# A GRU over gathered item rows: 12 raw steps in place of 10, a ring of 16 steps in place of 12

## The chip, the cores and the metric

The kernel runs on one core of one Trainium2 chip. The metric is the device time of one execution in microseconds. Three runs of the kernel before took 1093.35, 1089.58 and 1090.4 us, so the median is 1090.4 us. Engines are named as in the profile: PE is TensorE (PEld its weight loads), DVE is VectorE, ACT is ScalarE, POOL is GpSimd, SP is SyncE.

## The reference

512 sequences of 200 item numbers go through one GRU layer of width 128 and then through a dense layer with softmax over 100 classes. The item table has 12,500 rows of 128 floats.

```python
x = emb[item_seq]                       # [512, 200, 128], f32
mask = item_seq != 0
def step(h, x_t, m_t):
    mx = x_t @ W + b_i                  # W, U: [128, 384]
    mh = h @ U + b_r
    z = sigmoid(mx[:, :D] + mh[:, :D])
    r = sigmoid(mx[:, D:2*D] + mh[:, D:2*D])
    hh = tanh(mx[:, 2*D:] + r * mh[:, 2*D:])
    return where(m_t, z * h + (1 - z) * hh, h)
# 200 steps in order, h starts at 0
softmax(h_last @ Wout + bout)
```

## The kernel before

The batch of 512 is four blocks of 128. Blocks 0 and 1 are chain 0, blocks 2 and 3 chain 1, and the two chains take turns on the engines. The state of a chain is a tile of 128 x 256 floats, features by sequences. A step needs, for every sequence, the row of its item.

The work has three stages.

1. **Building two tables in DRAM.** SP loads the transposed item table into the SBUF tile `arena`. PE turns it back tile by tile (L323), ACT and DVE copy the tiles to `turned`, and SP stores them as `rows` (item rows of 128 floats, L210 to L216). PE also multiplies each tile by W (L318), ACT and DVE copy the products to `proj` (L453, L517), and SP stores them as `table` (rows of 384 floats, already multiplied by W, L221 to L230). A mask is built in: item 0 points at a row that pins the update gate.
2. **Raw steps**, t = 0 to RAW - 1. They use `rows`, which is complete before `table` is. POOL gathers 128 rows per block with an indirect DMA (L284, 4 per step) into the tile `raw`. PE transposes them (L351), ACT copies the result to `xT` (L474), and PE multiplies by W for the three gates (L358, L359, L362) and adds the pin (L365).
3. **Table steps**, t = RAW to 199. POOL gathers rows of `table` (L302, 4 per step, each 128 rows of 384 floats) into `arena`, which by then serves as a ring of RING steps. PE transposes the rows straight into the sums of the three gates (L377, 12 transposes per step); no multiplication by W is left.

In both kinds of step PE multiplies the state by U (L383 reset gate, L385 candidate, L389 update gate), ACT computes r (L478), z (L480) and the candidate (L482), and DVE does five operations per chain (L541, L544, L546, L549, and L552, which writes the new `h`).

Every engine has its own instruction stream in program order, and semaphores join them. What orders the work around the change is POOL's stream: its 4 x RAW raw gathers, then one wait for all stores of `table` (L289 to L291), then the gathers for the table steps. Table step number n = t - RAW uses ring slot n % RING. From n = RING on, POOL waits until PE has transposed the rows that the slot held before:

```python
if n >= RING:
    pool.wait_ge(s_free[c], n - RING + 1)
```

A raw step and a table step share the semaphore of a slot, so for n < RAW the table gather also waits for the raw gather of the same number (L301).

POOL's stream is written out for all steps. On PE, ACT and DVE the table steps are a loop of TURNS = (200 - RAW) // RING turns of RING steps, and the LEFT remaining steps stand behind it: 15 turns and 10 steps before.

Of the kernel before, what the change touches and what calls it, by code (L numbers as in the profile page):

```python
# [14 lines left out]

CHAINS = ((0, 1), (2, 3))
WIDTH = 2 * P
RAW = 10
RING = 12
CHUNK = 8  # L20
HALF = CHUNK // 2
GROUP = 4
# [5 lines left out]
def gru(nc: bass.Bass, item_seq, emb_cols, W, U, b_i, b_r, Wout, bout, out):  # L28
# [17 lines left out]
    CLASSES = Wout.shape[1]  # L46
    assert D == P and GATES == 3 * D and BATCH == BLOCKS * P and 1 <= RAW <= RING
    TURNS = (STEPS - RAW) // RING
    LEFT = STEPS - RAW - TURNS * RING
    BOTH = range(len(CHAINS))  # L50
# [6 lines left out]
    assert TILES == CHUNKS * CHUNK + 1 and TILES == GROUPS * GROUP + 1 and 0 < REST < P  # L57
    assert ITEMS <= RING * BLOCKS * GATES

# [5 lines left out]
    with ExitStack() as ctx:  # L65
        def sb(name, shape, dt=F32):
            return ctx.enter_context(nc.sbuf_tensor(name, shape, dt))

        def sem(name):
            return ctx.enter_context(nc.semaphore(name))  # L70

        def per_chain(name):
            return [sem(f"{name}{c}") for c in BOTH]
# [3 lines left out]

        arena = sb("arena", [P, RING * BLOCKS * GATES])
        raw = sb("raw", [P, RAW * BLOCKS * D])
        turned = [sb(f"turned{q}", [P, CHUNK, D]) for q in range(STAGES)]  # L80
# [15 lines left out]
        SEQS = BLOCKS * STEPS  # L96
        assert 4 * SEQS <= RAW * BLOCKS * D

# [7 lines left out]
        copy_f = sb("copy_f", [P, 1])  # L106
        masked = sb("masked", [P, RAW * BLOCKS], BF16)
        pins = sb("pins", [P, P], BF16)
# [59 lines left out]

        s_slot = [[sem(f"slot{s}_block{k}_gathered") for k in range(BLOCKS)] for s in range(RING)]
        s_x = per_chain("x_turned")  # L170
# [439 lines left out]
```

## Time and profile before

| | us |
|---|---|
| median of three runs | 1090.4 |
| profiled execution, its own time | 1093.43 |
| its span, first to last instruction | 1091.6 |
| outside the span (1093.43 - 1091.6) | 1.83 |
| POOL busy in the span | 803.7 |
| PE busy in the span | 981.0 |
| first raw gather, first table gather, last table gather (starts) | 40.19, 99.88, 1074.58 |

The profile gives each engine's busy time and the idle time ahead of its instructions. A busy share is no proof that an engine sets the pace: PE's share is the highest, but it is a mean over stretches in which different things come last. One gather is two times: how long POOL needs to issue it (the duration of the instruction), and how long until its rows have landed (another view gives that).

### The profile page before, as it was taken

The page shows a single profiled execution, that of the slowest core. Times are in us where ns is not written, and L with a number is a line of the kernel's source. Part 1 is how long each engine was busy: PE and PEld are TensorE (multiplying, and loading weights), DVE is VectorE, ACT ScalarE, POOL GpSimd, SP SyncE. Part 2 cuts the span into 40 slices and gives each one's busy share as a digit, 9 for nine tenths or more (in the row PEclk, how much of TensorE's full clock was granted, in tenths as well). Part 3 has the DMA queues.
Part 4 walks back from the last instruction along what each step waited for, and adds up shares of the span by engine and source line. Part 5 has one row for each costly group of instructions (what it writes and reads, how often), then busy time and mean ns, then how long its engine had stood idle before and what let it go on. Part 6 is the DMA issues. An engine that isn't in the chain of part 4 may idle for free.

```text
span 1091.6 us, 15880 instructions
## 1 busy us (share of the span) xinstructions
PE 981.0 (90%) x5185; PEld 756.4 (69%) x5185; DVE 862.6 (79%) x2074; ACT 577.7 (53%) x1288; POOL 803.7 (74%) x820
## 2 busy tenths in 40 slices
PE   6899999999999999999999999888888888888885
PEld 5556887777777777777777776666666666666664
DVE  3344778888888888888888888888888888888886
ACT  3334655555555555555555555555555555555554
POOL 6574777777777777777777777777777777777773
PEclk9899999999999999999999999999999999999998
DMA  9997555555555555555555555555555555555552
GB/s 359 378 360 262 159 157 153 153 152 154 151 155 152 153 153 153 154 152 152 153 156 152 153 152 154 153 152 151 154 152 155 153 153 154 153 152 154 152 155 81
DMA packets 59696, 185.75 MB, mean 170 GB/s; under 512 B 14830, under 2 KB 16408, under 8 KB 59672
## 3 DMA queue, kind: packets, MB, share of 16 engines
q0 software_dynamic: 49920, 152.09, 49.4%
q1 hardware_dynamic: 8356, 32.47, 7.5%
q10 hardware_dynamic: 1396, 0.91, 0.3%
q8 instruction: 9, 0.15, 0.1%
q14 instruction: 15, 0.12, 0.0%
HBM read 159.35 MB, written 26.07 MB: 170 GB/s over the span
## 4 chain that ended last, share of the span: by engine, by line
DVE 29%; DMA 23%; PE 16%; issue 12%; ACT 11%; POOL 9%; DVEq 0%; SPq 0%; POOLq 0%; ACTq 0%
DMA arena<-table,row_table 21%; ACT cand L482 10%; DVE rh L541 10%; POOL arena L302 9%; DVE zc L549 9%; DVE pre L544 9%; PE bank L318 5%; PE bank L377 4%; DMA rows<-turned 1%; PE bank L383 1%; DVE h L552 1%; PE bank L389 1%; PE bank L385 1%; PE bank L358 1%; PE bank L362 1%
## 5 line engine op out<-in xcount | busy, mean ns | idle before, releaser
L302 POOL DMA_INDIRECT arena<-table,row_table x760 | 744.4, 979 | 241.0 <-issue 178.2
L377 PE MATMUL bank<-ident,arena 128*128 128x128 f32 x2280 | 346.5, 277 | 64.3 <-DMA arena<-table,row_table 63.9
L377 PEld LDWEIGHTS bank<-ident,arena 128*128 128x128 f32 x2280 | 269.4, 141 | 141.6 <-DMA arena<-table,row_table 103.0
L482 ACT ACTIVATE cand<-pre,bi 128x256 f32<-128x256 f32 x400 | 203.3, 508 | 280.4 <-DVE pre L544 280.4
L383 PE MATMUL bank<-h,U_sb 128*128 128x256 f32 x800 | 261.6, 409 | 22.5 <-DVE h L552 4.9
L549 DVE SCALAR_TENSOR_TENSOR zc<-z,cand 128x256 f32<-128x256 f32 x400 | 171.2, 428 | 92.9 <-ACT cand L482 92.9
L389 PE MATMUL bank<-h,U_sb 128*128 128x256 f32 x800 | 239.3, 381 | 0.0
L385 PE MATMUL bank<-h,U_sb 128*128 128x256 f32 x800 | 238.6, 380 | 0.0
L478 ACT ACTIVATE r<-bank,b_gates 128x256 f32<-128x256 f32 x400 | 185.1, 463 | 83.3 <-PE bank L383 82.2
L541 DVE SCALAR_TENSOR_TENSOR rh<-bank,br,r 128x256 f32<-128x256 f32 x400 | 191.8, 479 | 44.6 <-ACT r L478 34.2
L480 ACT ACTIVATE z<-bank,b_gates 128x256 f32<-128x256 f32 x400 | 189.3, 473 | 69.8 <-PE bank L389 69.8
L552 DVE TENSOR_TENSOR h<-zh,zc 128x256 f32<-128x256 f32 x400 | 172.9, 432 | 13.8
L544 DVE TENSOR_TENSOR pre<-rh,bank 128x256 f32<-128x256 f32 x400 | 168.2, 420 | 13.8
L383 PEld LDWEIGHTS bank<-h,U_sb 128*128 128x128 f32 x800 | 120.1, 190 | 74.0 <-DVE h L552 73.9
L546 DVE TENSOR_TENSOR zh<-z,h 128x256 f32<-128x256 f32 x400 | 169.7, 424 | 0.4 <-ACT z L480 0.4
L385 PEld LDWEIGHTS bank<-h,U_sb 128*128 128x128 f32 x800 | 152.4, 190 | 20.7
L389 PEld LDWEIGHTS bank<-h,U_sb 128*128 128x128 f32 x800 | 137.3, 190 | 37.6 <-DVE pre L544 3.1
L318 PE MATMUL bank<-W_sb,arena 128*128 128x384 f32 x198 | 70.5, 510 | 3.7 <-ACT proj L453 3.7
L318 PEld LDWEIGHTS bank<-W_sb,arena 128*128 128x128 f32 x198 | 38.6, 201 | 28.5 <-ACT proj L453 4.4
L517 DVE COPY proj<-bank 128x384 f32<-128x384 f32 (+1 forms) x49 | 27.2, 557 | 39.0 <-PE bank L318 33.7
L284 POOL DMA_INDIRECT raw<-rows,row_table x40 | 38.0, 950 | 20.2 <-issue 11.9
L453 ACT COPY proj<-bank 128x384 f32<-128x384 f32 x50 | 23.8, 479 | 45.0 <-PE bank L318 39.1
(55 smaller groups left out, 165.8 us busy)
## 6 DMA issues: line engine op xcount, KB each, us to landing
table<-proj SPq DMA_DIRECT2D x24, 768.0 KB, 3.9
arena<-table,row_table POOLq DMA_INDIRECT x760, 3.1
arena<-in_L_rec_emb SPq DMA_DIRECT2D x12, 512.0 KB, 10.1
rows<-turned SPq DMA_DIRECT2D x12, 512.0 KB, 10.7
raw<-rows,row_table POOLq DMA_INDIRECT x40, 4.0
seq<-in_r_item_seq ACTq DMA_DIRECT2D x1, 400.0 KB, 10.3
table<-proj SPq DMA_DIRECT2D x2, 192.0 KB
out_probs<-probs SPq DMA_DIRECT2D x1, 200.0 KB, 2.6
```

The source lines that it names most:

```text
L302: pool.indirect_dma_start(ring_rows(s, k), None, table, bass.IndirectOffsetOnAxis(row_table[:, t, k:k + 1], 0)).then_inc(s_slot[s][k], 16)
L377: last = pe.matmul(dst[:, i * P:(i + 1) * P], ring_row(s, k, g), ident[:, :], start=(i == 0), stop=False, is_transpose=True, skip_group_ch ...
L383: pe.matmul(reset_sum[c], U_sb[:, D:2 * D], h[c][:, :], start=False, stop=True, skip_group_check=True).then_inc(s_reset[c], 1)
L385: pe.matmul(cand_h[c], U_sb[:, 2 * D:3 * D], h[c][:, :], start=False, stop=True, skip_group_check=True).then_inc(s_cand[c], 1)
L389: pe.matmul(update_sum[c], U_sb[:, 0:D], h[c][:, :], start=False, stop=True, skip_group_check=True).then_inc(s_update[c], 1)
L478: act.activation(r[c][:, :], reset_sum[c], ACT.Sigmoid, bias=b_gates[:, 1:2]).then_inc(s_r[c], 1)
L480: act.activation(z[c][:, :], update_sum[c], ACT.Sigmoid, bias=b_gates[:, 0:1]).then_inc(s_z[c], 1)
L482: act.activation(cand[c][:, :], pre[c][:, :], ACT.Tanh, bias=bi[:, 2:3]).then_inc(s_tanh[c], 1)
L541: dve.scalar_tensor_tensor(out=rh[c][:, :], in0=cand_h[c], scalar=br[:, 2:3], in1=r[c][:, :], op0=ALU.add, op1=ALU.mult).then_inc(s_rh[c], 1)
L544: dve.tensor_tensor(pre[c][:, :], rh[c][:, :], cand_x[c], ALU.add).then_inc(s_pre[c], 1)
L549: dve.scalar_tensor_tensor(out=zc[c][:, :], in0=z[c][:, :], scalar=1.0, in1=cand[c][:, :], op0=ALU.subtract, op1=ALU.mult).then_inc(s_zc[c ...
L552: dve.tensor_tensor(h[c][:, :], zh[c][:, :], zc[c][:, :], ALU.subtract).then_inc(s_h[c], 1)
```

## The change

RAW goes from 10 to 12 and RING from 12 to 16. Two constants change, and everything else follows from them.

```diff
-RAW = 10
-RING = 12
+RAW = 12
+RING = 16
```

Steps 10 and 11 become raw steps: 48 raw gathers in place of 40, and 752 table gathers in place of 760. `raw` grows from 20 to 24 KB per partition and `arena` from 72 to 96 KB. The loop on PE, ACT and DVE has 11 turns of 16 steps and 12 steps behind it.

On POOL, the number of gathers of each kind at the end of the index work and behind it (`raw` and `arena` are the targets, `rows` and `table` the two tables):

```order
 L269 TENSOR_TENSOR raw<-raw 128x800
 L272 TENSOR_TENSOR raw<-raw 128x800
 L274 CAST row_table<-raw 128x800
-L284 DMA raw<-rows,row_table 128x128 x40
-L302 DMA arena<-table,row_table 128x384 x760
+L284 DMA raw<-rows,row_table 128x128 x48
+L302 DMA arena<-table,row_table 128x384 x752
 L65 UNCONDITIONAL_BRANCH
```

Eight gathers move from behind the wait for the table's stores to ahead of it; the total stays 800.

On POOL, where the first gathers that wait for a free ring slot stand (`rows_transposed0` and `1` are PE's signals that a chain's rows have been transposed). Before:

```order
L302 DMA arena<-table,row_table 128x384 [waits slot9_block3_gathered]
L302 DMA arena<-table,row_table 128x384 x8
L302 DMA arena<-table,row_table 128x384 [waits rows_transposed0]
L302 DMA arena<-table,row_table 128x384
L302 DMA arena<-table,row_table 128x384 [waits rows_transposed1]
```

And now:

```order
L302 DMA arena<-table,row_table 128x384 [waits slot11_block2_gathered]
L302 DMA arena<-table,row_table 128x384 [waits slot11_block3_gathered]
L302 DMA arena<-table,row_table 128x384 x16
L302 DMA arena<-table,row_table 128x384 [waits rows_transposed0]
L302 DMA arena<-table,row_table 128x384
L302 DMA arena<-table,row_table 128x384 [waits rows_transposed1]
```

The first 48 table gathers (40 that wait for a raw gather and 8 that wait for nothing) were free of the wait for a slot; now the first 64 are (48 and 16).

On PE, at the end of the raw steps, the first half of the first added raw step (each of the two steps has two such halves, one per chain):

```order
 L362 MATMUL bank<-xT,W_sb 128x256
 L365 MATMUL bank<-pins,masked 128x128 x2
+L351 MATMUL bank<-ident,raw 128x128 x2
+L383 MATMUL bank<-h,U_sb 128x256
+L385 MATMUL bank<-h,U_sb 128x256
+L389 MATMUL bank<-h,U_sb 128x256
+L358 MATMUL bank<-xT,W_sb 128x256
+L359 MATMUL bank<-xT,W_sb 128x256
+L362 MATMUL bank<-xT,W_sb 128x256
+L365 MATMUL bank<-pins,masked 128x128 x2
```

Two steps of PE's work change from six transposes and three multiplications per chain to the form above, so PE reaches the first table step later by what a raw step takes, twice.

## Rows read from the trace of the kernel before

**Rows 1.** The page: span, busy time and count of each engine.

```profile
span 1091.6 us, 15880 instructions
PE 981.0 (90%) x5185; PEld 756.4 (69%) x5185; DVE 862.6 (79%) x2074; ACT 577.7 (53%) x1288; POOL 803.7 (74%) x820
```

**Rows 2.** Waits of POOL: waiting line, releaser, us in total, times, longest us.

```profile
POOL arena L302 <- issue: 178.2, 585, 0.3
POOL arena L302 <- PE bank L377: 53.0, 174, 0.3
POOL arena L302 <- DMA table<-proj: 9.8, 1, 9.8
```

**Rows 3.** Timeline of POOL: start, us, line, operation, [idle before, releaser].

```profile
85.40 0.94 POOL L284 DMA_INDIRECT raw<-rows,row_table  x1 [0.30 <-issue]
...
89.15 0.94 POOL L284 DMA_INDIRECT raw<-rows,row_table  x1 [0.30 <-issue]
99.88 0.95 POOL L302 DMA_INDIRECT arena<-table,row_table  x1 [9.79 <-DMA table<-proj]
...
160.29 0.95 POOL L302 DMA_INDIRECT arena<-table,row_table  x1 [0.30 <-issue]
...
1074.58 0.95 POOL L302 DMA_INDIRECT arena<-table,row_table  x1 [0.30 <-issue]
```

**Rows 4.** Line 302 by itself: count, durations, first and last start; landing times.

```profile
L302 POOL DMA_INDIRECT arena<-table,row_table x760: 942/946/1197, 99.9 to 1074.6; - x190
...
DMA to landing us min/median/max: 2.9/3.1/4.8
```

**Rows 5.** Stretches of PE's line 377: stretch, length, busy (count), PEclk, DMA, GB/s.

```profile
155.00:660.00 505.00, 177.68 (x1302) 155.37 (x1302) 1.00 0.54 153
680.00:1060.00 380.00, 153.18 (x886) 102.94 (x886) 1.00 0.54 153
```

**Rows 6.** The same two stretches, POOL alone.

```profile
155.00:660.00 505.00, 385.40 (x393) 1.00 0.54 153
680.00:1060.00 380.00, 290.12 (x296) 1.00 0.54 153
```

**Rows 7.** Chain that ended last, in order of time, around 664 us.

```profile
663.55 0.84 PE bank L377 x6
...
664.46 0.95 POOL arena L302
...
665.71 3.06 DMA arena<-table,row_table
```

**Rows 8.** Timeline of DVE's line 552, the new state.

```profile
108.33 0.42 DVE L552 TENSOR_TENSOR h<-zh,zc 128x256 f32<-128x256 f32 x1
...
155.19 0.45 DVE L552 TENSOR_TENSOR h<-zh,zc 128x256 f32<-128x256 f32 x1
...
160.26 0.49 DVE L552 TENSOR_TENSOR h<-zh,zc 128x256 f32<-128x256 f32 x1
...
269.68 0.49 DVE L552 TENSOR_TENSOR h<-zh,zc 128x256 f32<-128x256 f32 x1
272.25 0.42 DVE L552 TENSOR_TENSOR h<-zh,zc 128x256 f32<-128x256 f32 x1
...
1081.29 0.43 DVE L552 TENSOR_TENSOR h<-zh,zc 128x256 f32<-128x256 f32 x1
```

**Rows 9.** Timeline of PE, the first and the last table transposes.

```profile
156.06 0.82 PE L377 MATMUL bank<-ident,arena 128*128 128x128 f32 x6
...
1071.86 0.90 PE L377 MATMUL bank<-ident,arena 128*128 128x128 f32 x3 [2.31 <-DMA arena<-table,row_table]
...
1079.01 0.82 PE L377 MATMUL bank<-ident,arena 128*128 128x128 f32 x6
```

**Rows 10.** Stretches, all engines (PE, PEld, DVE, ACT, POOL), around the table's last stores.

```profile
40.00:90.00 50.00, 48.26 (x141) 28.17 (x142) 19.96 (x36) 17.59 (x37) 37.91 (x40) 0.93 0.93 355
90.00:100.00 10.00, 8.91 (x35) 5.54 (x34) 2.85 (x6) 3.39 (x8) 0.21 (x2) 1.00 0.80 302
```

## The prediction

> **What bounds the kernel now.** I read the page first, then POOL's waits, POOL's timeline, and one pair of stretches on PE and POOL. By the page PE is busiest (90%) and POOL third (74%) [rows 1], which by itself would make PE the suspect. POOL's waits say otherwise. Ahead of its 760 table gathers POOL idles in three ways: 585 times for "issue", 178.2 us in all, that is 0.305 us each; 174 times with PE named as releaser, 53.0 us, that is also 0.305 us each and never over 0.3; and once for the table's stores, 9.8 us [rows 2]. A gap that is the same with and without a releaser is POOL's own gap between two gathers, so no gather ever waited for a ring slot. POOL issues one gather after the other from 99.88 to 1074.58 us: (1074.58 - 99.88) / 759 = 1.284 us each [rows 3]. The only hole in its stream of 800 gathers is the wait for the stores.
>
> PE's pace and POOL's pace are close, and the stretches tell which is slower. There are 12 transposes of line 377 in a step, so from 155 to 660 us a step takes 505 / (1302 / 12) = 4.65 us, and from 680 to 1060 us 380 / (886 / 12) = 5.15 us [rows 5]. POOL needs 4 x 505 / 393 = 5.14 us for the gathers of a step in the first stretch and 4 x 380 / 296 = 5.14 us in the second [rows 6]. POOL is thus the slower one all the way. At first PE eats up the lead that POOL gained during the raw steps; at 664 us the lead is gone, the chain that ends last goes over from PE to gathers and their landings [rows 7], and from there PE's step is POOL's. The end of the kernel is therefore the time at which POOL may begin with table gathers, plus their number times 1.284 us, plus a tail.
>
> **The change part by part.**
>
> *Eight more raw gathers ahead of the wait.* The raw gathers from 85.40 to 89.15 us stand (89.15 - 85.40) / 3 = 1.25 us apart [rows 3]. The last one of before starts at 89.15; eight more start from 90.40 to 99.15, and POOL is ready for the first table gather at 100.40 us. Before, the stores released it at 99.88. So the eight fill the hole of 9.79 us (0.30 of which is the usual gap) and overrun it by 0.52 us. If the stores land later because of them, that counts only from 100.40 on; rival B prices it.
>
> *Eight fewer table gathers behind it.* 8 x 1.284 = 10.27 us. From both parts the last gather starts 10.27 - 0.52 = 9.75 us sooner, at 1064.83 us. Landing, the last steps and the softmax (1091.6 - 1074.58 = 17.0 us) stand behind the last gather in both kernels, and I cost them as equal.
>
> *Two raw steps in place of table steps on PE, ACT and DVE.* From the second to the tenth raw step the new state of chain 0 comes every (155.19 - 108.33) / 8 = 5.86 us [rows 8], against 4.65 us of a table step. Two steps cost 2 x 1.21 = 2.42 us. POOL's slower pace hides them. Had PE kept 4.65 us from step 10 (state at 160.26 us) to step 199, that state would come at 160.26 + 189 x 4.65 = 1039.1 us; it came at 1081.29 [rows 8], so PE has 42.2 us to spare. After the change it has 42.2 - 2.4 - 9.75 = 30.0 us. If POOL stopped setting the pace, the 2.42 us would count in full.
>
> *The ring of 16.* In the kernel before it buys nothing, since no gather waited for a slot. With 12 raw steps it is needed. The first gather that waits for a slot is the 49th, at 160.29 us [rows 3], and PE clears the first slot at 156.06 + 0.82 = 156.88 us [rows 9], 3.4 us ahead. Two more raw steps move the clearing to 156.88 + 2 x 5.86 = 168.6 us. With 12 slots POOL would come to the 49th gather at about 100.40 + 160.29 - 99.88 = 160.8 us and stand for 7.8 us, most of the gain. With 16 slots the first gather that waits is the 65th, at about 160.8 + 16 x 1.284 = 181.3 us, 12.7 us behind the clearing. So the ring is worth zero by itself and keeps 7.8 us here. In later steps PE is faster than POOL and the margin only grows.
>
> *Other edits.* The mask for 12 steps has 48 columns in place of 40 and lies ahead of the wait for the item rows: nothing. A loop of 11 turns in place of 15 saves four jumps back; at a jump the state of one chain comes 272.25 - 269.68 = 2.57 us after the other's in place of about 4.65 / 2 = 2.33 [rows 8], so four jumps are 1.0 us of PE's time, which POOL's pace hides. What a loop body longer by a third costs at the jump, no row shows: between -1.0 us (four jumps fewer, were PE the bound) and rival A's price. I take 0, the side of the nearest row, since the present body of 12 x 12 transposes and more jumps for 0.24 us.
>
> The Trainium skill (Runtime: NRT & Kernel Launch, Instruction fetch mechanics) says that a taken branch to a target outside the fetched window of instructions makes the engine wait for a fetch. The row on the jump, 0.24 us, shows no such wait; by the row the sum stays as it is, by the rule it becomes rival A's.
>
> *Sum.* 1093.43 - 9.75 = 1083.7 us for an execution like the profiled one, which is 3.0 us above the median of the runs (1090.4) and close to the slowest of them. The difference applied to the median: 1090.4 - 9.75 = 1080.6 us.
>
> **The rivals.**
>
> *A, slower: the longer loop body is fetched anew at each jump.* One mechanism on PE, ACT or DVE, 11 times. It begins to show only when it uses up the 30.0 us to spare, at 30.0 / 11 = 2.7 us per turn, and makes the kernel slower by over 0.3% (3.3 us) from (30.0 + 9.75 + 3.3) / 11 = 3.9 us per turn. As its price I take the longest landing of a transfer in the rows, 4.8 us [rows 4]: 11 x 4.8 - 30.0 = 22.8 us, and 1080.6 + 22.8 = 1103 us. For it: 12 steps have been shown to be cheap, 16 have not. Against it: the 0.24 us. Chance 0.05.
>
> *B, smaller gain: the added gathers delay the stores.* From 90 to 100 us the DMA engines moved 302 GB/s at a share of 0.80, from 40 to 90 us 355 GB/s at 0.93 [rows 10]. Eight gathers bring 8 x 128 x 512 bytes = 0.52 MB into that stretch, 52 GB/s over 10 us, which makes 354 and uses up what was free. At worst the last store lands later by all of it, 0.52 MB / 355 GB/s = 1.5 us: release at 101.4 us, 1.0 us behind 100.40, gain 8.75, time 1081.7 us. At best nothing moves, since 354 is still below the 355 that was reached. Chance 0.11.
>
> The Trainium skill (DMA: Bandwidth & Descriptors, Issuing engines are not separate DMA queues) says that DMAs started by different engines run on the same 16 DMA engines and interleave. The two stretches agree in that gathers and stores together stayed near 355 GB/s; by the rows the sum stays, and by the rule taken alone B's 1 us comes off the gain.
>
> *C, no change: what POOL gives back early is lost at a new wait.* Say the gathers of the two added steps land late and the table gathers of slots 10 and 11, which now wait for them, hold POOL; or gathers slow down in the wider `arena`: 10 us over 752 gathers would take 0.013 us each, less than their spread of 942 to 1197 ns [rows 4]. Time 1090.4 us. Against it: those waits come 40 gathers, about 50 us, after the raw gathers were issued, and landings take 3.1 us in the median. Chance 0.07.
>
> A small gain beside these belongs to the forecast's own range. Near the end one gather's rows let PE wait 2.31 us, and PE's last transposes start at 1079.01 us, though the last gather could have landed at 1074.58 + 3.1 = 1077.7 us [rows 3, 4, 9]. If that late landing is chance and does not come again, the end is up to 1.3 us earlier.
>
> **How the numbers follow.** Forecast 0.77, A 0.05, B 0.11, C 0.07. Forecast 1080.6 us. Its own range goes down to 1077.5 (the 1.3 us, and 1.8 for the spread of the runs) and up to 1083.7 (an execution like the profiled one). With B and its spread the range is 1077.5 to 1085.0; A and C, 0.12, stay outside. A difference under 0.3% of the time, 3.3 us, cannot be told from no change. Faster: 0.77 + 0.11 = 0.88; same: 0.07; slower: 0.05.
>
> **What would show it.** After the change POOL's idle time ahead of its first table gather should be about 0.3 us (up to 1.3 under B) in place of 9.79, that gather should start at 100.4 us (to 101.4), and the spacing of table gathers should stay at 1.284 us. The chain should go over to gathers later: POOL's lead at a given step is greater by 9.75 + 2.42 = 12.2 us, PE closes 5.14 - 4.65 = 0.49 us per step, 25 steps or 116 us, so near 664 + 2 + 116 = 782 us. The last table gather should start near 1065 us. The prediction is wrong if POOL stands anywhere for a slot or a landing, if gathers come more than 1.29 us apart, or if PE waits for anything but gathers in the last 200 us.

## The result: 1081.7 us after 1090.0 us, as POOL's hole was filled

The changed kernel took 1081.68 us in the median (1080.71 to 1082.67, four runs), the kernel before 1090.0 us beside it; the ratio is 0.9917, 95% interval 0.9895 to 0.9939, so the change is small but clear of no change. Measured once more beside the experiments it was 1082.19 us against 1091.67, ratio 0.9909 (0.9893 to 0.9926). The forecast was 1080.6 us, range 1077.5 to 1085.0.

The profiled execution of the changed kernel took 1081.61 us. The first lines of its page, which answer to [rows 1]:

```profile
span 1079.8 us, 15857 instructions
PE 982.1 (91%) x5201; PEld 757.4 (70%) x5201; DVE 860.4 (80%) x2074; ACT 571.7 (53%) x1292; POOL 804.8 (75%) x820
```

The busy times hardly differ. What changed is where POOL stands idle. Its waits in the changed kernel (waiting line, releaser, us in total, times, longest), to be read against [rows 2]:

```profile
POOL arena L302 <- issue: 186.1, 611, 0.3
POOL arena L302 <- PE bank L377: 42.9, 141, 0.3
```

The third row of before, the 9.8 us for the table's stores, has no successor. POOL's timeline, against [rows 3] (start, us, line, operation, [idle before, releaser]):

```profile
39.26 1.20 POOL L284 DMA_INDIRECT raw<-rows,row_table  x1 [7.28 <-DMA rows<-turned_last]
...
98.19 0.94 POOL L284 DMA_INDIRECT raw<-rows,row_table  x1 [0.30 <-issue]
99.44 1.07 POOL L302 DMA_INDIRECT arena<-table,row_table  x1 [0.31 <-issue]
...
1065.22 0.95 POOL L302 DMA_INDIRECT arena<-table,row_table  x1 [0.30 <-issue]
```

The first table gather follows the last raw gather after 0.31 us, POOL's usual gap, and the last gather starts 9.36 us sooner than before. Line 377 on PE, against [rows 5] (stretch, length, PE busy (count), PEld busy (count), PEclk, DMA share, GB/s), and the place where the chain that ends last goes over to gathers, against [rows 7] (start, us, what):

```profile
166.00:730.00 564.00, 198.74 (x1458) 173.88 (x1457) 1.00 0.53 153
790.00:1010.00 220.00, 88.63 (x513) 59.73 (x513) 1.00 0.53 153
```

```profile
740.90 0.76 PE bank L377 x6
741.85 0.95 POOL arena L302
743.10 3.23 DMA arena<-table,row_table
```

PE still takes 564 / (1458 / 12) = 4.64 us for a step while it has a lead to eat up, and 220 / (513 / 12) = 5.15 us once it works on each gather as it lands. The lead lasts until 742 us in place of 664.

### The profile page after: what moved, and what is told of

It is laid out like the page before. It is cut to its first block, busy times and chain, and to the rows that moved or that the text cites. A ratio compares the mean times of both kernels' runs of the same rounds, so it can differ in the third digit from the quotient of the medians.

```text
span 1079.8 us, 15857 instructions
## 1 busy us (share of the span) xinstructions
PE 982.1 (91%) x5201; PEld 757.4 (70%) x5201; DVE 860.4 (80%) x2074; ACT 571.7 (53%) x1292; POOL 804.8 (75%) x820
## 4 chain that ended last, share of the span: by engine, by line
DVE 33%; DMA 19%; PE 16%; ACT 13%; issue 12%; POOL 6%; DVEq 0%; SPq 0%; POOLq 0%; ACTq 0%
DMA arena<-table,row_table 16%; ACT cand L482 12%; DVE rh L541 11%; DVE zc L549 10%; DVE pre L544 10%; POOL arena L302 6%; PE bank L318 5%; PE bank L377 3%; DMA rows<-turned 1%; PE bank L383 1%; DVE h L552 1%; PE bank L389 1%; PE bank L385 1%; PE bank L358 1%; PE bank L359 1%
## 5 line engine op out<-in xcount | busy, mean ns | idle before, releaser
L377 PE MATMUL bank<-ident,arena 128*128 128x128 f32 x2256 | 334.5, 276 | 49.4 <-DMA arena<-table,row_table 49.3
L318 PE MATMUL bank<-W_sb,arena 128*128 128x384 f32 x198 | 67.6, 494 | 1.5 <-ACT proj L453 1.5
L284 POOL DMA_INDIRECT raw<-rows,row_table x48 | 45.5, 949 | 21.6 <-issue 14.3
## 6 DMA issues: line engine op xcount, KB each, us to landing
rows<-turned SPq DMA_DIRECT2D x12, 512.0 KB, 10.4
seq<-in_r_item_seq ACTq DMA_DIRECT2D x1, 400.0 KB, 10.4
```

The costliest lines, as they stand in the source:

```text
L377: last = pe.matmul(dst[:, i * P:(i + 1) * P], ring_row(s, k, g), ident[:, :], start=(i == 0), stop=False, is_transpose=True, skip_group_ch ...
```

## The experiments

Theory: POOL's stream of 800 gathers sets the end. Its length without holes is fixed, so the time is the start of the stream, plus that length, plus any hole, plus a tail. Rivals: the deeper ring or the shorter count of loop turns gives the gain; each raw step saves its table gathers without limit; PE sets the end.

Start, hole, last gather, stream and tail are from the one profiled execution of each kernel, the medians from all its runs (us). Each ratio is to the kernel before as it ran in the same group: 1090.0 us for the changed kernel, 1091.0 for the next four, 1091.67 for the four after them, 1091.63 for the last two.

| kernel | first gather | hole | last gather | stream less hole | tail | median | ratio (95%) |
|---|---|---|---|---|---|---|---|
| before, 10 raw, ring 12 | 40.19 | 9.49 | 1074.58 | 1024.9 | 17.0 | 1090.0 | |
| changed, 12 raw, ring 16 | 39.26 | 0 | 1065.22 | 1026.0 | 14.6 | 1081.68 | 0.9917 (0.9895 to 0.9939) |
| 12 raw, ring 12 | 39.59 | 6.58 | 1072.88 | 1026.7 | 17.4 | 1088.93 | 0.9979 (0.9968 to 0.999) |
| 10 raw, ring 16 | 39.80 | 8.26 | 1075.39 | 1027.3 | 14.5 | 1091.79 | 1.0002 (0.9991 to 1.0013) |
| 11 raw, ring 16 | 40.21 | 4.17 | 1070.88 | 1026.5 | 14.5 | 1085.23 | 0.9941 (0.9925 to 0.9957) |
| 14 raw, ring 15 | 39.37 | 0 | 1066.09 | 1026.7 | 15.7 | 1083.64 | 0.9933 (0.9917 to 0.9949) |
| the change again | 39.31 | 0 | 1064.32 | 1025.0 | 14.9 | 1082.19 | 0.9909 (0.9893 to 0.9926) |
| 12 raw, ring 14 | 40.25 | 0 | 1067.42 | 1027.2 | 15.4 | 1083.88 | 0.9924 (0.9909 to 0.9939) |
| rows given | 32.30 | 0 | 1057.45 | 1025.2 | 15.5 | 1075.79 | 0.9858 (0.9838 to 0.9878) |
| rows given, index on DVE | 21.54 | 3.10 | 1049.88 | 1025.2 | 15.1 | 1066.81 | 0.9766 (0.9748 to 0.9783) |
| the same, 14 raw, ring 18 | 22.54 | 0 | 1048.20 | 1025.7 | 14.8 | 1065.63 | 0.9762 (0.9749 to 0.9776) |
| the change, loop ends early | 39.55 | 0 | 1064.67 | 1025.1 | 14.9 | 1081.43 | 0.9909 (0.9894 to 0.9924) |

The hole is the idle time less the usual gap of 0.30 us; the tail is the span less the start of the last gather. In the twelve profiles the stream without its hole took 1024.9 to 1027.3 us, or 1.283 to 1.286 us a gather; what makes this spread of 2.4 us, no run shows.

**12 raw steps with the ring of 12** (the ring part undone).

```diff
-RING = 16
+RING = 12
```

> 12 raw steps with the old ring of 12. Theory (POOL's stream of 800 gathers without a hole sets the end, and the ring of 16 only keeps it free of a hole): the 49th table gather, due near 160.1 us, waits for the first slot, which PE clears near 164.7 us, so a hole of 4 to 9 us opens on POOL there and the kernel takes 1086 to 1090 us. Rival (the ring is idle, the raw steps give the whole gain): no hole, 1081.7 us as with the change.

POOL's timeline at the 49th table gather, and PE's transposes that clear the first slot:

```profile
159.13 0.94 POOL L302 DMA_INDIRECT arena<-table,row_table  x1 [0.30 <-issue]
166.95 0.94 POOL L302 DMA_INDIRECT arena<-table,row_table  x1 [6.88 <-PE bank L377]
168.20 0.95 POOL L302 DMA_INDIRECT arena<-table,row_table  x1 [0.30 <-issue]
```

```profile
165.86 0.82 PE L377 MATMUL bank<-ident,arena 128*128 128x128 f32 x6
```

The hole of the kernel before is gone at 99.8 us and comes back at 160 us, 6.88 us long, released within 0.3 us of the end of PE's first transposes. Most of the gain goes with it: 1088.93 us. The raw steps alone are worth 0.2%.

**10 raw steps with the ring of 16** (the ring part alone), **11 raw steps** (half of the raw part) and **14 raw steps** (twice the raw part, with 15 slots, which fit).

```diff
-RAW = 12
+RAW = 10        # then 11, and 14 with RING = 15
```

> 10 raw steps with the ring of 16. Theory: no gather ever waited for a slot, so nothing changes, 1090 us (within 0.3%), with a hole of 6 to 10 us ahead of the first table gather. Rival (the deeper ring or the fewer jumps of the loop give the gain): 1082 us. Rival (a loop body of 16 steps costs a fetch per turn): over 1093 us.

> 11 raw steps, ring of 16. Theory: four gathers fill half of the hole, so the gain is four table gathers, 4 x 1.286 = 5.1 us: 1085 us (1083.5 to 1087, since the hole varies with the time at which the table's stores land). Rival (the gain comes only with a full fill or only from the ring): 1090 or 1082 us.

> 14 raw steps, ring of 15 (16 slots do not fit in SBUF beside them). Theory: the hole is full already, POOL's 800 gathers take the same time in any mix, and PE's two longer steps (2.4 us) are hidden: 1081.7 us within 0.2%, first table gather near 109.4 us and last near 1065 us. Rival 1 (each pair of raw steps saves its eight table gathers): 1071.5 us. Rival 2 (PE's longer raw steps are paid in full): 1084 us.

The wait for the table's stores with 10 and with 11 raw steps, and line 302 by itself with 14 (count, shortest, median and longest in ns, first and last start):

```profile
POOL arena L302 <- DMA table<-proj: 8.6, 1, 8.6
```

```profile
POOL arena L302 <- DMA table<-proj: 4.5, 1, 4.5
```

```profile
L302 POOL DMA_INDIRECT arena<-table,row_table x744: 942/947/1198, 109.8 to 1066.1; - x186
```

The ring alone leaves the hole at 8.6 us and the time where it was (1.0002). Four gathers leave a hole of 4.5 us and give 0.6%, eight give 0.8 to 0.9%, and sixteen give 0.7%, no more than eight: with 14 raw steps the first table gather starts 10.4 us later than with 12 and the last 0.9 us later. Rival 1 of that run (1071.5 us) is out. Its 1083.64 us was 2 us above the changed kernel; the intervals overlap, so whether the two longer steps of PE or the later table gathers cost anything is not settled by the times, but the profile shows no wait of POOL over 0.3 us.

**The change again, and 12 raw steps with a ring of 14.**

```diff
-RING = 16
+RING = 14
```

> The change once more, as the measure for the others of this group. Theory: ratio 0.991 to 0.994 to the kernel before (eight gathers of 1.286 us fewer behind the stores, less what the hole falls short of ten microseconds), so 1082 us. In the profile again one late landing of 4.6 to 4.9 us after the loop's end, with a block of instructions of 16 KB on the DMA engines in the same stretch.

> 12 raw steps, ring of 14. Theory: the first gather that waits for a slot is the 57th, due at 99.4 + 56 x 1.257 = 169.8 us, 5 us after PE clears the slot at 164.7 us, so 14 slots are enough: no hole, the same time as the change within 0.2%. Rival (each slot fewer costs something): half way between 12 and 16 slots, 1085 us.

With 14 slots no gather waits (longest idle of POOL at line 302: 0.3 us), as the 57th gather comes after the slot is clear. The time was 1.7 us above that of 16 slots in the same group (1083.88 and 1082.19), with overlapping intervals. In the profiles the stream started 0.94 us later and was 2.2 us longer, without any hole; that lies within the spread of the column in the table above. Whether two slots fewer cost anything below this spread is open.

**An earlier start of the stream.** If start plus length is the time, an earlier start must pay in full. In the first of two versions the item rows come as an input in row layout, with the zero row and the copies of the last row behind them; turning the table and storing `rows` fall away, and the raw gathers need to wait only for the index work. In the second the index work runs on DVE between the copies of the products. The cut shows the first lines of each part only.

```diff
-def gru(nc, item_seq, emb_cols, W, ...):
+def gru(nc, item_seq, emb_cols, rows, W, ...):
-            for q in range(STAGES):
-                pool.wait_ge(s_rows[q], 16 * len(range(q, CHUNKS, STAGES)))
-            pool.wait_ge(s_rows_last, 16 * 3)
...
-            pool.tensor_copy(item_f, seq[:, :, :]).then_inc(s_idx, 1)
+                dve.tensor_copy(item_f, seq[:, :, :]).then_inc(s_idx, 1)
```

> The change, with the item rows (and the zero row and the 128 copies of the last row) handed over as a further input in row layout, so that the kernel neither turns the table back nor stores the rows; index work stays on POOL. Theory: POOL's stream starts where the index work ends, near 32 us in place of 39.3, and the end moves by the same 7.3 us: 1074.5 us (1073 to 1076). Rival (the end is set by PE, which gets its table earlier by some 20 us): over 10 us less, 1065 us. Rival (the start of the stream does not matter since the stores release it): 1081.7 us.

> As the one with the rows given, and the index work moved from POOL to DVE, between the copies of the products. Theory: the stream starts near 20 to 24 us, 15 to 19 us before that of the change, and the end moves by as much: 1063 to 1067 us; PE keeps some 40 us to spare. Rival (another engine becomes the bound or the stores, now released later than the raw gathers end, open a hole): 1068 to 1074 us.

Line 278 of the first and line 255 of the second version are the table gathers; the third and fourth rows are POOL's long waits in the second:

```profile
L278 POOL DMA_INDIRECT arena<-table,row_table x752: 942/946/1193, 92.7 to 1057.5; - x188
```

```profile
L255 POOL DMA_INDIRECT arena<-table,row_table x752: 942/946/1198, 84.8 to 1049.9; - x188
...
POOL raw L237 <- DVE row_table L469: 19.5, 1, 19.5
...
POOL arena L255 <- DMA table<-proj: 3.4, 1, 3.4
```

The first starts its stream 7.0 us before the change (32.30 and 39.31) and its last gather 6.9 us before it; the time fell by 6.4 us to 1075.79. The second starts 17.8 us earlier, opens a hole of 3.1 us beyond the gap, and its last gather comes 14.4 us earlier; the time fell by 15.4 us to 1066.81, 2.3% below the kernel before. PE is still not the bound: apart from the hole POOL never waits over 0.3 us.

**14 raw steps and a ring of 18 in that version**, to fill its new hole.

```diff
-RAW = 12
-RING = 16
+RAW = 14
+RING = 18
```

> The version with the rows given and the index work on DVE, with 14 raw steps and a ring of 18, for which there is room now. In that version POOL waits 3.4 us again for the table's stores. Theory: eight more raw gathers fill this hole, POOL issues its 800 gathers in one piece, and the end moves by the hole, 3.1 us (3.4 less the usual gap of 0.3): 1063.7 us within 0.2%. Rival (the next two raw steps save their eight table gathers): 1056.5 us. Rival (no further gain, since something else ends last): 1066.8 us.

```profile
22.54 1.13 POOL L237 DMA_INDIRECT raw<-in_rows,row_table  x1 [20.49 <-DVE row_table L469]
```

The hole is gone, but the row above shows that the stream of this execution began 1.0 us later, and the last gather came 1.7 us earlier, not 3.1. The median, 1065.63 us, is the lowest of all; against the version before it the runs do not tell a difference (ratios 0.9762 and 0.9766 with overlapping intervals). Both beat the changed kernel.

**The loop left one turn earlier**, for the late landing told of below.

```diff
-            with eng.Fori(0, TURNS) as turn:
+            with eng.Fori(0, TURNS - 1) as turn:
                 one_turn(turn, RING)
+            one_turn(TURNS - 1, RING)
             one_turn(TURNS, LEFT)
```

> The change with the last turn of the loop written out behind it, so that PE, ACT and DVE leave the loop at step 172 in place of step 188. Theory on the late landing (blocks of instructions that the engines fetch once they have left the loop hold up one DMA engine): the first step of PE over 6 us after the raw steps comes 16 steps earlier, at steps 173 to 182, near 930 to 990 us, with a block of 16 KB in the same stretch. Rival (it belongs to the end of the run or to the number of gathers): again at steps 189 to 198. On the time: the same as the change within 0.2%, 1082 us, since POOL's stream is the same.

The time stayed (1081.43 us), and the first long step of PE came at step 173 in place of 189; three more followed at steps 183, 189 and 194. What this shows stands in the last section.

## Why the prediction was right

*What bounds the kernel.* Right. Ring alone 1.0002, raw steps alone 0.9979, a start of the stream 7.0 us earlier giving 6.4 us: POOL's stream sets the end, and neither PE's busy share (90%) nor the wait on free slots does. Nor does the amount of data: in the kernel before a raw gather, with a third of the bytes of a table gather, kept POOL as long (median 944 and 946 ns). Why some gathers take up to 1.2 us to issue, so that the mean spacing is 1.286 us and not 1.25, no run shows.

*Eight gathers in the hole.* Forecast: first table gather at 100.40 us, spacing 1.284 us, last gather at 1064.83. Measured: 99.44, (1065.22 - 99.44) / 751 = 1.286, and 1065.22. The stream itself began 0.93 us earlier than before (39.26 and 40.19).

*The size of the hole* was taken from one execution, and there it was large. In that execution PE had a mean granted clock of 0.93 from 40 to 90 us [rows 10]; in the changed kernel the same stretch shows 1.00:

```profile
40.00:90.00 50.00, 49.19 (x153) 29.05 (x154) 21.66 (x39) 19.02 (x40) 37.81 (x41) 1.00 0.97 377
```

PE then finished the table earlier: its first raw step began at 92.60 us in place of 96.46, and the last store was issued at 92.85 in place of 96.62. The other seven profiles of kernels that build both tables agree: at 1.00 the last store was issued at 92.8 and 93.2 us, at 0.97 between 94.5 and 95.4. With the 3.26 us that went from the last issue to the release before (99.88 - 96.62), the stores of a kernel before with that clock would release POOL near 96.1 us (an estimate), so the raw gathers overran this by 3.3 us and not by 0.52. Beside such a kernel the gain is 8 x 1.286 - 3.3 = 7.0 us; with stores as late as in the profile it is the 9.75 us of the forecast. The measured differences of the medians, 8.3 and 9.5 us, lie between. The sign did not hang on it, the size did, by about a quarter. So it is in part luck that the median came within 1.1 us of the forecast: the profiled execution of before was the slowest of its four, and the gain worked out from its hole was taken off the median of all.

*Two raw steps on PE are hidden.* Right: PE kept 4.64 us a step and no time was lost to it. The hand-over at 742 us came before the forecast 782 for the same reason as above. PE's raw steps began 3.9 us earlier, which took 3.9 us from POOL's lead; at 0.49 us a step these are 8 steps or 37 us. In the change's second profile, with a clock of 0.97 in that stretch, PE's raw steps began 2.1 us earlier than before, and the hand-over came near 772 us.

*The ring of 16.* Right, and the term that the diff alone does not show. With 12 slots the forecast hole was 7.8 us at the 49th gather; 6.6 us beyond the usual gap were measured (PE's first clearing at 166.7 us in place of the estimated 168.6). With 14 slots there was none.

*Rival A, the longer loop body.* Not there. The state of a chain after a jump back, in the changed kernel:

```profile
314.65 0.48 DVE L552 TENSOR_TENSOR h<-zh,zc 128x256 f32<-128x256 f32 x1
317.20 0.43 DVE L552 TENSOR_TENSOR h<-zh,zc 128x256 f32<-128x256 f32 x1
319.52 0.42 DVE L552 TENSOR_TENSOR h<-zh,zc 128x256 f32<-128x256 f32 x1
```

The states of the two chains take turns: 2.55 us pass at the jump against 2.32 after it, so the jump costs 0.23 us, as with 12 steps (0.24). All ten jumps back lie between 220 and 1010 us, and in that stretch the DMA queues moved the gathers and six packets of instructions on q14, and none on q8, which carries 16 KB packets of instructions before and after it (packets, MB, share of 16 engines):

```profile
q0 software_dynamic: 39241, 120.60, 52.9%
q14 instruction: 6, 0.05, 0.0%
```

The q14 packets are fewer than the jumps. The rule that the prediction cited from the Trainium skill (Runtime: NRT & Kernel Launch, Instruction fetch mechanics), that a taken branch out of the fetched window waits for a fetch, does not show in these loops of 12 to 18 steps; whether their jumps leave that window, no run shows.

*Rival B, later stores.* There, but without a cost. SP's stores run on DMA queue q1. The last 0.2 us in which q1 moves packets of them are 99.2 to 99.4 us before and 96.4 to 96.6 us in the changed kernel (before, then changed: packets, MB, share of 16 engines):

```profile
q1 hardware_dynamic: 2, 0.00, 2.3%
```

```profile
q1 hardware_dynamic: 3, 0.00, 4.3%
```

From the last store's issue this is at most 2.8 us before (issue at 96.62) and 3.75 us in the changed kernel (92.85), so beside the added gathers the stores took about 0.9 us longer. With 11 raw steps, where the stores still release POOL, the release came 4.2 us after the last issue; with 10 it came after 3.3, with either ring. In the changed kernel the stores' last packets had moved some 2.8 us before POOL came to its first table gather at 99.44, so the delay cost nothing. The prediction's comparison of stretches for this rival was loose: of the two in [rows 10] only the first (355 GB/s) has gathers and stores together; in the second, 302 GB/s, POOL was busy for 0.21 us.

*Rival C, a new wait.* Not there: no idle time of POOL ahead of a table gather is over 0.31 us. The 3.1 us that the prediction set against it is the landing of table gathers; raw gathers landed in 4.0 us in the median before and 4.9 in the changed kernel, at most 6.7, still far below the 50 us.

*The tail, costed as equal,* was not: 17.0 us before, 14.6 after. The span fell by 11.8 us: 9.5 by the hole and 0.9 by the earlier start, less 1.1 by which the stream without its hole was longer, and 2.4 by this tail. It is the late landing of which the prediction said that up to 1.3 us might go, and the clock that fell after it, which the prediction did not count. The late landing did not go away, it came earlier (last section). How much of the gain of the medians is tail cannot be told, since only one execution of before was profiled.

## What to carry to other kernels

An engine with a middling busy share can set the time if it never stops: compare its idle gaps with its own smallest gap, and look for the one that is longer. Where a stream of fixed length is the bound, only its start and its holes can be moved; work taken from behind a wait to ahead of it pays until the hole is full, and not beyond (4, 8 and 16 gathers: 0.6%, 0.8 to 0.9%, 0.7%). And when a producer gets a head start, check that the ring behind it is deep enough for the lead: here the ring gave nothing by itself and kept most of the gain.

## What the runs showed of the hardware

**A late gather, and a block of instructions beside it.** In eleven of the twelve profiles PE waits 1.5 to 2.4 us for a gather in one or a few steps near the end, which then take longer than the others (8.19 us before, at step 197; 8.07 in the changed kernel, at step 189). The longest landing of a table gather is 4.6 to 5.0 us in these kernels; the median is 3.1 or 3.0. In the changed kernel, PE around that step, and the stretches about it on PE, PEld, DVE, ACT and POOL with PEclk, DMA share and GB/s:

```profile
1019.08 0.70 PE L377 MATMUL bank<-ident,arena 128*128 128x128 f32 x3 [2.27 <-DMA arena<-table,row_table]
1019.58 1.06 PE L383 MATMUL bank<-h,U_sb 128*128 128x256 f32 x2
...
1023.10 0.60 PE L383 MATMUL bank<-h,U_sb 128*128 128x256 f32 x2
```

```profile
1012.00:1018.00 6.00, 4.34 (x24) 3.46 (x24) 4.88 (x13) 3.42 (x7) 4.48 (x5) 1.00 0.55 158
1018.00:1021.00 3.00, 1.92 (x7) 1.65 (x8) 0.60 (x2) 0.32 (x1) 2.39 (x3) 0.72 0.55 150
1021.00:1024.00 3.00, 3.00 (x15) 2.52 (x14) 1.98 (x5) 1.29 (x4) 2.39 (x3) 0.71 0.56 153
```

The DMA queues from 1013 to 1019 us (packets, MB, share of 16 engines):

```profile
q0 software_dynamic: 283, 0.91, 55.0%
q8 instruction: 1, 0.02, 1.7%
```

If one DMA engine carried the packet of instructions, it took 0.017 x 16 x 6 = 1.6 us of it, about what the landing was late (4.8 less 3.1). In the changed kernel no packet stands on q8 from 220 us until PE, ACT and DVE have left the loop: with the loop left 16 steps earlier, the first long step moved from step 189 to step 173 (state of the two chains, and the wait of PE; lines of that kernel are one further on):

```profile
930.86 0.42 DVE L553 TENSOR_TENSOR h<-zh,zc 128x256 f32<-128x256 f32 x1
933.32 0.42 DVE L553 TENSOR_TENSOR h<-zh,zc 128x256 f32<-128x256 f32 x1
935.83 0.42 DVE L553 TENSOR_TENSOR h<-zh,zc 128x256 f32<-128x256 f32 x1
940.36 0.42 DVE L553 TENSOR_TENSOR h<-zh,zc 128x256 f32<-128x256 f32 x1
```

```profile
936.80 0.55 PE L378 MATMUL bank<-ident,arena 128*128 128x128 f32 x3 [2.36 <-DMA arena<-table,row_table]
```

There, too, a packet of instructions stands in the trace just ahead, between 932 and 934 us. Not every packet does it: behind the loop q8 shows three in the changed kernel, of which one comes with a wait of over 1 us, and six with the loop left earlier, of which four do (the last packet of either kernel comes after the last gather). That the packet sits on the same DMA engine as the late part of the gather was not shown, so that it delays the gather is argued and not shown.

**The clock after a wait.** In the changed kernel PE idled 2.27 us at that step, and in the next two stretches its mean granted clock was 0.72 and 0.71 in place of 1.00: its matmuls took 1.06 us a pair at the lower of its two levels, 1.2 GHz, for about 4 us, then 0.60 again. A wait of that length is not enough: with the loop left earlier PE waited 2.36 us, and its clock stayed at 1.00 (the stretch behind that wait, in the order of the stretches above):

```profile
938.00:941.00 3.00, 3.00 (x21) 2.67 (x21) 2.30 (x6) 2.01 (x5) 2.19 (x3) 1.00 0.50 149
```

In the change's second profile it stayed at 1.00 as well, after 2.07 us. What decides it is open. Before the change the clock fell among the last steps, after the wait of 2.31 us:

```profile
1071.00:1074.00 3.00, 2.14 (x7) 1.88 (x8) 0.37 (x1) 0.35 (x1) 2.39 (x3) 0.61 0.56 159
```

The two profiles in which matmuls of the last three steps ran at the lower level, this one and that of 12 raw steps with the ring of 12, have the longest tails (17.0 and 17.4 us; the others 14.5 to 15.7). In the changed kernel it fell at step 189, and the tail was 14.6 us.
